# Broadcast of three rstd pairs by DMA through DRAM, the b2 product as one rounded pass, and gate transposes behind the down product

## The reference

```python
xw = x @ Wx + b
h[t+1] = tanh(xw[:, t] + h[t] @ Wh)                  # 32 steps, each on 32 sequences
xf = hs.reshape(-1, 128)                             # 1024 tokens
xn = xf * rsqrt(mean(xf * xf, -1) + 1e-5) * norm_scale
vals, idx = top_k(xn @ wg + bg, 4)                   # 16 experts, 4 chosen
gate_full = sum_k one_hot(idx_k) * softmax(vals)_k
h2 = xn @ w1[e] + b1[e]                              # for every expert e
a, g = min(h2[::2], 7), clip(h2[1::2], -7, 7)
s = a * sigmoid(1.702 * a) * (g + 1)
t = sum_e gate_full[:, e] * (s @ w2[e] + b2[e])
out = x + (hs + t)
```

## Time and profile before

| | |
|---|---|
| timed executions, us | 109.71, 110.6, 113.1 (median 110.6) |
| profiled execution, us | 110.22 |
| its span, first to last instruction, us | 108.4 |
| TensorE busy | 102.9 us, 95% |
| VectorE, ScalarE, GpSimd busy | 64.6, 60.8, 63.8 us |
| DMA | 12.94 MB |

### The profile page before, as it was taken

How to read it: one execution, slowest core, us unless ns; L and a number is a source line. 1 busy time by engine, 2 the same in 40 slices (tenths; PEclk the granted TensorE clock), 3 DMA queues, 4 the chain that set the end, 5 groups by cost and what they waited for, 6 DMA issues and landing times.

```text
span 108.4 us, 1718 instructions
## 1 busy us (share of the span) xinstructions
PE 102.9 (95%) x562; PEld 87.0 (80%) x562; DVE 64.6 (60%) x173; ACT 60.8 (56%) x139; POOL 63.8 (59%) x76
## 2 busy tenths in 40 slices
PE   7899999999999999999999969999999999999980
PEld 2557689988899999999989958886888888888760
DVE  0101367876818976399747996578266656666730
ACT  5144826899646486767716645665364566645400
POOL 3004348987791996449980799896444466545400
PEclk9999999999999999999999999999999999999999
DMA  2997930007930002991058814991000000000012
GB/s 77 235 335 266 398 113 0 0 6 234 390 159 3 0 0 74 296 379 39 12 165 246 308 60 116 336 361 59 6 0 0 0 3 0 0 0 0 0 48 48
DMA packets 4936, 12.94 MB, mean 119 GB/s; under 512 B 752, under 2 KB 1728, under 8 KB 4928
## 3 DMA queue, kind: packets, MB, share of 16 engines
q1 hardware_dynamic: 4704, 12.67, 34.7%
q10 hardware_dynamic: 224, 0.17, 0.6%
HBM read 12.25 MB, written 0.59 MB: 118 GB/s over the span
## 4 chain that ended last, share of the span: by engine, by line
PE 79%; DVE 9%; ACT 5%; DMA 2%; issue 1%; DVEq 0%
PE psA L774 19%; PE psB L774 17%; PE psY L804 10%; PE psR L804 5%; PE psR L722 5%; PE psM L804 5%; PE psY L722 2%; DMA wx_x_sb<-in_wx_x 2%; PE psA L751 2%; PE psM L729 2%; PE psR L714 2%; ACT psA L483 2%; PE psR L816 2%; ACT psA L492 2%; PE psM L816 2%; DVE lin L667 1%
## 5 line engine op out<-in xcount | busy, mean ns | idle before, releaser
L406 POOL TENSOR_TENSOR actg<-act,gate_cols 128x512 f32<-128x512 f32 x31 | 39.4, 1279 | 13.7 <-DVE act L682 12.9
L667 DVE TENSOR_SCALAR lin<-psB,one_b1b 128x256 f32<-128x256 f32 (+1 forms) x48 | 26.0, 569 | 23.3 <-PE psB L774 23.3
L483 ACT ACTIVATE psA<-psA,lim_b1a 128x256 f32<-128x256 f32 (+1 forms) x48 | 23.8, 515 | 26.5 <-PE psA L774 26.5
L682 DVE SCALAR_TENSOR_TENSOR act<-lin,psA 128x512 f32<-128x512 f32 x32 | 21.9, 686 | 1.8 <-ACT psA L492 0.5
L492 ACT ACTIVATE psA<-psA,limit_col 128x512 f32<-128x512 f32 x32 | 21.1, 660 | 0.8
L774 PE MATMUL psA<-xn_hi,w_hi 128*128 128x256 f32 (+1 forms) x48 | 20.5, 428 | 0.0
L804 PE MATMUL psY<-actg,w_sb 128*128 128x256 f32 x64 | 17.1, 389 | 0.0
L774 PE MATMUL psB<-xn_hi,w_hi 128*128 128x256 f32 (+1 forms) x48 | 16.0, 332 | 0.0
L774 PE MATMUL psA<-xn_hi,w_lo 128*128 128x256 f32 (+1 forms) x48 | 15.8, 328 | 0.0
L774 PE MATMUL psB<-xn_lo,w_hi 128*128 128x256 f32 (+1 forms) x48 | 15.6, 325 | 0.0
L774 PE MATMUL psB<-xn_hi,w_lo 128*128 128x256 f32 (+1 forms) x48 | 15.5, 323 | 0.0
(11 more groups left out here) (82 smaller groups left out, 136.0 us busy)
## 6 DMA issues: line engine op xcount, KB each, us to landing
gate_cols<-gate_rows SPq DMA_DIRECT2D x16, 512.0 KB, 6.0
w_sb<-in_w SPq DMA_DIRECT2D x4, 512.0 KB, 8.0
w_sb<-in_w SPq DMA_DIRECT2D x4, 256.0 KB, 9.3
out<-yT SPq DMA_DIRECT2D x3, 128.0 KB, 1.7
wx_x_sb<-in_wx_x SPq DMA_DIRECT2D x1, 320.0 KB, 6.0
wx_x_sb<-in_wx_x SPq DMA_DIRECT2D x2, 128.0 KB, 2.5
small_h<-in_small ACTq DMA_DIRECT2D x1, 105.0 KB, 2.7
gate_rows<-gT SPq DMA_DIRECT2D x4, 16.0 KB, 1.4
```

The costliest lines, as they stand in the source:

```text
L406: nc.gpsimd.tensor_tensor(by_pair(actg[:, u % SUM_DEPTH, w]), by_pair(act[:, u % ACT_DEPTH, w]), gate_block(u, w), ALU.mult).then_inc(actg ...
L483: last = nc.scalar.activation(psA[u % 2][:, o], psA[u % 2][:, o], ACT.Relu, scale=-1.0, bias=lim_b1a[:, e0 + k:e0 + k + 1])
L667: last = nc.vector.tensor_scalar(lin[:, v % 2, o], psB[v % 2][:, o], one_b1b[:, e0 + k:e0 + k + 1], LIMIT + 1.0, ALU.add, ALU.min)
L682: nc.vector.scalar_tensor_tensor(act[:, v % ACT_DEPTH, 0:w], lin[:, v % 2, 0:w], 1.0 - LIMIT, psA[v % 2][:, 0:w], ALU.max, ALU.mult).then_ ...
```

## The change

Pairs 1 to 3 no longer use TensorE for spreading rstd. SP writes the pair's `rstd` (128 partitions by 2) to DRAM and reads it back with one 128 KB broadcast transfer into `rstd_cols`, ahead of the gate transfers of the same pair. VectorE's `normalise` for these pairs waits for this transfer, reads `rstd_cols` instead of psM, and stands one unit later (`NORMAL` = 7, 11, 15), with GpSimd's `xn_low`.

`b2` is loaded five times below itself (80 rows), on ScalarE's queue behind `small`. VectorE makes a rounded copy and, in the last 16 rows, a remainder. The gates are written three times side by side, 80 columns wide with zeros between, so that the transposes give 80 rows; ScalarE makes a second, rounded copy `gS`, VectorE replaces 16 rows of it by the remainder (`gates_low`), and one float32r product with 80 rows of contraction takes the place of the float32 product.

From unit 7 on the gate transposes stand behind the down product of their unit. The filler products between the steps of the head are gone (five of 512 columns at the start stay); the logits of tile 0 move between steps, and the product of x and Wx for tiles 3 and 4 becomes two products, one in front of `lay_rstd(1)`. The last four units' down products are split 384 and 128 columns instead of 256 and 256, with the additions and the stores split alike, and the first half of the last one waits for both gate products.

```diff
@@ -41,7 +41,7 @@
...
     NU = UNIT0[NC]
-    WARM, WARM_START, WARM_GAP = 512, 5, 256
+    WARM, WARM_START = 512, 5
     LAG = 4
...
@@ -62,11 +62,14 @@
...
     RSTD = [None] + [v + 1 for v in STATS[1:]]
+    NORMAL = [None] + [v + 3 for v in STATS[1:]]
     GATES, GATES_T = [[k] + [v + 2 + k for v in STATS[1:]] for k in (0, 1)]
...
     EQ = E // GATE_GROUPS
+    GR = 5 * E
+    LOW_AT = 32
...
@@ -90,7 +93,8 @@
...
         bg_sb = sb("bg_sb", [P, E])
-        b2_sb = sb("b2_sb", [E, H])
+        b2_sb = sb("b2_sb", [GR, H])
+        b2_w = sb("b2_w", [GR, H], F32R)
         w1_sb = sb("w1_sb", [H, E, 2, I])
...
@@ -234,9 +248,10 @@
...
-        def y_end_bank(k):
-            return psM if k else psR
+        def y_end(k):
+            o = [slice(0, 3 * P), slice(3 * P, W)][k]
+            return o, (psM if k else psR)[:, 0:o.stop - o.start]
...
@@ -284,7 +299,7 @@
...
                 g = pair_group(q)
-                later += [(STATS[q], 1, ("stats", g)), (RSTD[q], 2, ("rstd", g))]
+                later += [(STATS[q], 1, ("stats", g))]
             order += [k[2] for k in sorted(later, key=lambda k: k[:2])]
...
@@ -305,7 +320,6 @@
...
                 sp.dma_start(w2_sb[:, ge, :], w2[:, ge, :]).then_inc(w2_loaded[g], 16)
-            sp.dma_start(b2_sb[:, :], b2).then_inc(b2_loaded, 16)
...
@@ -320,13 +334,24 @@
...
+            def spread_rstd(q):
+                sp.wait_ge(rstd_ready, pair_group(q) + 1)
+                sp.dma_start(rstd_rows[q, :, :],
+                             rstd[:, 2 * q:2 * q + 2]).then_inc(rstd_written, 16)
+                sp.wait_ge(rstd_written, 16 * q)
+                sp.dma_start(rstd_cols[:, q, :], rstd_rows[q, :, :].rearrange("p j -> (p j)")
+                             .partition_broadcast(P)).then_inc(rstd_loaded[q], 16)
             for q in range(NQ):
+                if q:
+                    spread_rstd(q)
                 spread_gates(q)
...
             for k in range(2):
-                o = slice((NT - 4 + 2 * k) * P, (NT - 2 + 2 * k) * P)
+                o = slice((NT - 1) * P if k else (NT - 4) * P, NT * P if k else (NT - 1) * P)
                 sp.wait_ge(yT_ready, NC + k)
...
@@ -349,6 +374,7 @@
...
             nc.gpsimd.memset(expo[:, :, 0:1], 1.0)
+            nc.gpsimd.memset(gates_w[:, :, :], 0.0)
             nc.gpsimd.iota(iota_e[:, :], pattern=[[1, E]], base=0, channel_multiplier=0,
...
@@ -417,7 +443,7 @@
...
             for v in range(NU - 1 + POOL_LAG):
-                for q in at(RSTD, v - 1):
+                for q in at(NORMAL, v):
                     xn_low(pair_group(q))
...
@@ -433,6 +459,7 @@
...
             acte.dma_start(small_h[:, 0:SM], small).then_inc(small_loaded, 16)
+            acte.dma_start(b2_sb[:, :], b2).then_inc(b2_loaded, 16)
             acte.wait_ge(ident_ready, 1)
...
@@ -455,7 +482,9 @@
...
                 acte.wait_ge(gates_mm, q + 1)
-                nc.scalar.activation(gT[:, q * PW:(q + 1) * PW], psX[0:E, 0:PW], ACT.Copy).then_inc(gT_ready, 1)
+                qc = slice(q * PW, (q + 1) * PW)
+                nc.scalar.activation(gT[:, qc], psX[0:E, 0:PW], ACT.Copy).then_inc(gT_ready, 1)
+                nc.scalar.activation(gS[:, qc], psX[0:GR, 0:PW], ACT.Copy).then_inc(gS_high, 1)
...
@@ -501,7 +530,7 @@
...
             acte.wait_ge(yT_ready, NC + 1)
-            store(acte, slice((NT - 2) * P, NT * P), slice(P // 2, P))
+            store(acte, slice((NT - 1) * P, NT * P), slice(P // 2, P))
...
@@ -531,18 +560,25 @@
...
+                if g >= CHUNKS[0]:
+                    q = group_tiles(g).start // 2
+                    dve.wait_ge(rstd_loaded[q], 16)
+                    nc.vector.scalar_tensor_tensor(xn[:, group_cols(g)].rearrange("p (j t) -> p j t", j=2),
+                                                   hT[:, group_cols(g, N)].rearrange("p (j t) -> p j t", j=2),
+                                                   b_col[:, 1:2],
+                                                   rstd_cols[:, q, :].rearrange("p (t j) -> p j t", j=2),
+                                                   ALU.mult, ALU.mult).then_inc(xn_full, 1)
+                    dve.wait_ge(xn_full, q)
+                    nc.vector.tensor_copy(xn_hi[:, group_cols(g)], xn[:, group_cols(g)]).then_inc(xn_hi_ready, 1)
+                    return
                 m = psM_turn(("rstd", g))
...
                 h, n = hT[:, group_cols(g, N)], psM[:, 0:len(group_tiles(g)) * P]
-                if g < CHUNKS[0]:
-                    nc.vector.scalar_tensor_tensor(xn_hi[:, group_cols(g)], h, b_col[:, 1:2], n, ALU.mult,
-                                                   ALU.mult).then_inc(xn_hi_ready, 1)
+                nc.vector.scalar_tensor_tensor(xn_hi[:, group_cols(g)], h, b_col[:, 1:2], n, ALU.mult,
+                                               ALU.mult).then_inc(xn_hi_ready, 1)
                 nc.vector.scalar_tensor_tensor(xn[:, group_cols(g)], h, b_col[:, 1:2], n, ALU.mult,
...
                 dve.wait_ge(m_read, m)
-                if g >= CHUNKS[0]:
-                    nc.vector.tensor_copy(xn_hi[:, group_cols(g)], xn[:, group_cols(g)]).then_inc(xn_hi_ready, 1)
-                    return
                 dve.wait_ge(xn_hi_ready, g + 1)
...
@@ -607,14 +643,31 @@
...
                 nc.vector.tensor_tensor(
-                    gates[:, ts, :], gate_sum[:, ts, :],
-                    inv[:, ts].rearrange("p (j o) -> p j o", o=1).to_broadcast([P, 2, E]),
+                    gates_w[:, ts, :].rearrange("p j (a b e) -> p j a b e", a=3, b=2)[:, :, :, 0, :],
+                    gate_sum[:, ts, :].rearrange("p j (a e) -> p j a e", a=1).to_broadcast([P, 2, 3, E]),
+                    inv[:, ts].rearrange("p (j a e) -> p j a e", a=1, e=1).to_broadcast([P, 2, 3, E]),
                     ALU.mult).then_inc(scale_done, 1)
+            def gates_low(q):
+                dve.wait_ge(gS_high, q + 1)
+                low, qc = slice(LOW_AT, LOW_AT + E), slice(q * PW, (q + 1) * PW)
+                nc.vector.tensor_tensor(gS[low, qc], psX[low, 0:PW], gS[low, qc].bitcast(F32),
+                                        ALU.subtract).then_inc(gS_ready, 1)
...
                 gates_scale(q)
+            def b2_parts():
+                dve.wait_ge(b2_loaded, 16)
+                mark(nc.vector.tensor_copy(b2_w[:, :], b2_sb[:, :]))
+                settled()
+                low = slice(GR - E, GR)
+                nc.vector.tensor_tensor(b2_w[low, :], b2_sb[low, :], b2_w[low, :].bitcast(F32),
+                                        ALU.subtract).then_inc(b2_ready, 1)
...
@@ -634,6 +687,7 @@
...
             nc.vector.tensor_scalar(one_b1b[:, :], b1_sb[:, E:2 * E], 1.0, None, ALU.add).then_inc(b1_ready, 1)
+            b2_parts()
             stats(0)
...
@@ -667,6 +721,8 @@
...
                     last.then_inc(lin_done, 1)
+                for q in at(GATES_T, v - 1):
+                    gates_low(q)
                 for q in at(STATS, v):
...
@@ -696,10 +752,10 @@
...
             for k in range(2):
-                dve.wait_ge(y_end, k + 1)
-                o = slice((NT - 4 + 2 * k) * P, (NT - 2 + 2 * k) * P)
-                nc.vector.tensor_tensor(yT[:, o], xT[:, o], y_end_bank(k)[:, 0:PW],
-                                        ALU.add).then_inc(yT_ready, 1)
+                dve.wait_ge(y_done, k + 1)
+                o, y = y_end(k)
+                o = slice((NT - 4) * P + o.start, (NT - 4) * P + o.stop)
+                nc.vector.tensor_tensor(yT[:, o], xT[:, o], y, ALU.add).then_inc(yT_ready, 1)
...
@@ -708,10 +764,10 @@
...
-            def x_wx(j, n):
+            def x_wx(j, n, start=True):
                 pe.wait_ge(x_loaded if j > 2 else x1_loaded if j else wx_x0_loaded, 16)
-                nc.tensor.matmul(xw_cols(j, n), wx_sb, xT[:, j * P:(j + n) * P], start=True, stop=True,
+                nc.tensor.matmul(xw_cols(j, n), wx_sb, xT[:, j * P:(j + n) * P], start=start, stop=True,
                                  skip_group_check=True)
...
@@ -731,7 +787,8 @@
...
-                for k, j in enumerate(ts):
+                for j in ts:
+                    k = j % 2
                     last = nc.tensor.matmul(bank[:, 16 + k * E:16 + (k + 1) * E], hT[:, N + j * P:N + (j + 1) * P],
...
@@ -745,7 +802,7 @@
...
-            def keep_warm(n, w=WARM_GAP):
+            def keep_warm(n, w=WARM):
...
@@ -753,9 +810,9 @@
...
                 if q:
-                    pe.wait_ge(gT_ready, q)
+                    pe.wait_ge(gS_ready, q)
                 for k, j in enumerate(pair_tiles(q)):
-                    last = nc.tensor.transpose(psX[0:E, k * P:(k + 1) * P], gates[:, j, :], ident[:, :])
+                    last = nc.tensor.transpose(psX[0:GR, k * P:(k + 1) * P], gates_w[:, j, 0:GR], ident[:, :])
                 last.then_inc(gates_mm, 1)
...
@@ -779,21 +836,21 @@
...
                     return [(slice(0, CHUNKS[c] * P), psY[:, 0:CHUNKS[c] * P])]
```

(55 more changed lines are left out.)

7 lines of the change are left out of this document (5 added, 2 removed).

## The result

The changed kernel took 117.47 us in the median (116.14 to 120.34, 4 runs), the kernel before beside it 110.17 (109.71 to 113.1, 4 runs). The ratio is 1.060 with a 95% interval of 1.054 to 1.067: slower by 6%, outside the forecast range of 108.2 to 112.6. Executions more than 1.5% above the fastest of their kernel, mostly those with a lower granted clock, are left out of every ratio, which is why this one is under the 1.066 of the two medians. The profiled execution took 116.14 us for a span of 114.4, the same 1.7 us around the span as before. So 6.0 us of span are to be found.

What follows compares the result with a forecast made beforehand. TensorE was taken as the bound, busy 102.9 of 108.4 us. Span 108.4 + 1.6 (wait) - 0.66 (chunk 2) - 0.2 (tail) = 109.15, with 1.8 around it 110.95, given as 110.9; range 108.2 to 112.6 us.

Steps and rivals of the forecast that it cites:

- The head: Head to unit 1: part of x by Wx runs earlier, the gS copy adds 0.27; net +0.1 us, summed as -0.1 gain.
- b2: Chunks 0, 1 and 2: one float32r product replaces the float32 product, gaining 0.3, 0.3 and 0.66 us.
- Transposes behind the down product: The two TensorE stops ending at 50.78 and 63.23: moving the gate transposes gains 0.1 us at both places.
- Sum up to unit 16 without the wait: TensorE up to unit 16: gains of 0.5 + 0.3 + 0.25 = 1.05 us, so a start at 63.4, before 64.48.
- the 0.25 of the last pair: Unit 13: two rstd transposes less on TensorE, 0.25 us at most.
- The tail: Last units: smaller last addition (0.13 us less) and a last store half as large, 0.2 us together.
- The new wait: Before unit 16: pair 3's rstd write lands after pair 2's gate columns drain, rstd_cols at 65.0; 1.6 us lost.
- Pair 2 has the same wait, shorter: Unit 11: rstd_cols at about 51.2, VectorE ready at 50.9 at the earliest; the loss is made up by unit 12.
- A: SP's rstd write overtakes the gate columns: unit 16 waits only 0.25 us for xn_lo; 108.5 us, chance 0.25.
- B: Head without fillers: the clock rises two units later, or idling before unit 16 does the same; 112.6 us, chance 0.15.
- C: Wait longer or repeated: rstd(2) holds the addition before chunk 1's product, 8-byte write adds 0.8; 1.3 more, 112.2 us, chance 0.1.
- D: The 80-row float32r product shows the old one's price: 1.2 us less gain, 111.7 us, chance 0.05.

Runs made afterwards that it cites:

- both edits: Changed kernel with the rstd write as one 1 KB piece and the read from 128 rows of x, other data than asked for: 111.17 us, one run.

## Why the prediction was wrong

*The parts of the gain.* *The head*: +0.1 net. The kernel with the old head equals the one without within the intervals, which neither bears out nor refutes 0.1. *b2*: 0.3, 0.3 and 0.66. Chunk 2 gave 0.82 in its products (0.84 + 0.22 became 0.18 + 0.06), more than 0.66, since the start cost that I kept was mostly not there. The two 0.3 brought unit 16 forward by nothing: it starts at 63.68 without the rounded pass too. *Transposes behind the down product*: 0.1, and nothing measurable came. *Sum up to unit 16 without the wait*: 63.4; with transposes, which keep the 0.25 of the last pair, it was 63.68. That this fits is luck in part, since 0.6 of the 1.05 us in the sum is b2. *The tail*: 0.2. From the tail's first product to the end of the span it was 108.4 - 101.64 = 6.76 us and is 114.4 - 108.02 = 6.38. 0.4, a little under-sized.

*The new wait* was the right mechanism, on the right queue and in the right order, but it was put at the wrong pair. What failed is one sentence: "Pair 2 has the same wait, shorter", `rstd_cols` "at about 51.2", and that what it loses "is made up by unit 12". It is 56.8. Of the 5.6 us between them, 2.4 are the write: I let it land when the gate columns had drained, but they were through soon after 50 and it landed at 52.66; its 128 pieces had a bound of 0.8 in pair 3's working and none here. 1.95 are the read, 4.15 where I took 2.2 from the 2.5 us row of a load with 128 rows of its own. That row was nearest by size, but it reads neither one row 128 times nor behind such a write, and each adds some 1 us. The remaining 1.2 is the drain itself: `gate_rows` of pair 1 landed after 3.4 us instead of 1.4, so the gate columns were issued at 43.23 instead of 41.86.

*What followed from it I had not followed.* VectorE was ready for `xn` of pair 2 at 51.8. With `rstd_cols` at 51.2 it waits for nothing; with 56.8 it waits 5.0, and the first product of chunk 1 came at 59.53 instead of the 54.0 of the text. The clock fell. And everything of pair 3 moved with it, its statistics and its `rstd` (ready at 61.78 where the text has 55.56), its routing and the gate products. So the wait that the forecast was built on, 1.6 us lost at `rstd_cols` of pair 3, hardly occurred: VectorE stood there for 0.15 us. Two paths end almost together before unit 16. The gate product ended at 70.44; `rstd_cols` of pair 3 landed at 66.25 + 3.8 = 70.05, which with `xn` and `xn_hi` makes 71.05. `xn_lo` needs both, so the second one decides, by 0.6 us. The kernel with pair 2 normalised late shows the forecast wait alone: there VectorE stands for 5.8 us at pair 3, whose `rstd_cols` land at 69.83 where the text has 65.0, and unit 16 starts at 70.72.

*Why the write is late* was put down to its place in SP's queue, and with it went the sentence of the Trainium skill, "DMA: Bandwidth & Descriptors", section "Queues, rings and completion order", on ring order. The write on ScalarE's empty queue was held for 6.3 us as well. Ring order may act on SP too, where the write took 7.6, but most of the hold is there without it. The same page's fixed cost and bandwidth ("Anatomy of one DMA", a fit that the page made on DMAs issued by GpSimd, where these are SP's) give 4.3 us for the round trip as an estimate. The emptiest one here, pair 1, took 2.7 + 4.3 = 7.0, and the form with one piece and own rows took 1.1 + 2.0 = 3.1. So the rule fits neither form. With the bytes the same, the pieces alone moved the round trip from 3.9 (1.1 + 2.8) to 7.0.

*The rivals.* A is refuted in two steps: the write is held up, and on an idle queue the round trip would have brought pair 3's `rstd_cols` at 55.7 + 0.7 + 7.0 = 63.4 and not at 60.0. B did not occur as told: the pace of the up products rose at 18.3 us, in the kernel before at 19.9. That the clock can fall over an idle stretch, which B adds for the stop before unit 16, did occur, one stop earlier; in other kernels of this case it occurred there too, and cost 2.9 us. C named what happened ("`rstd(2)` is late enough to hold the addition before chunk 1's product") and had the 0.8 for the pieces, but it was priced at 1.3 us where it cost 5.05 in the first stop and 7.4 by unit 16, and it had a chance of 0.1. D is refuted by the float32 variant (its own terms, 0.3 + 0.66 on top of 110.9, make 111.9 and not the 111.7 of the text). The range went wrong by the same sum: the upper bound came from one late pair, not from the second pair and the queue behind it.

## What to carry to other kernels

A small round trip through DRAM is not priced by its bytes: price it by its pieces, and by whether large transfers are in flight while it runs. Here 1 KB and 128 KB took 7 us on an idle queue and up to 12 beside 2 MB. The clock is a second price: a stop can cost some 3 us more in the products behind it than its own length. Before putting one into a loop, work out for each of its turns when it lands and what stands behind its wait on every engine in order, SP too; the turn that looked harmless here was the one that had less slack than its wait was long. And where a change has several parts, find the part that pays: here one product form gave 1.6% and the large part took 8 back.

## What the runs showed of the hardware

- A 1 KB write to DRAM landed after 1.1 us as one piece and 2.7 to 3.1 as 128 pieces of 8 bytes, and the 128 KB read behind it took 1.0 to 1.5 us longer when the write had been in pieces (4.3, 4.2, 3.8 against 2.8, 3.0, 2.8; 3.1 against 2.0), even where it read other data. Why the read is longer is open.
- A write issued within 2 us of 2 MB of gate columns took 5.8 to 7.9 us, whatever its form, and 6.3 and 5.9 from another engine's empty queue. Issued 3.5 to 5 us behind them it took 4.3 to 4.8.
- `gate_rows` of pair 1, 16 KB, landed after 1.4 us before, with transposes and in their three variants, and after 2.1 to 3.5 in the kernels with the DMA path. It isn't issued behind a large transfer there. Left open; that of pair 0 took about 3 us in three profiles, one of them with transposes, so the DMA path need not be the reason.
- The granted clock reads 1.00 in the head, where six up products take 1.30 us; in the one-piece kernel six take 1.28 in windows that read 0.50. The first up product at the faster pace begins between 17.9 and 20.5 us in the thirteen profiles without fillers in the head (18.6 in the changed kernel), and between 19.5 and 20.4 in the three with them, so the fillers don't bring it forward.
- After a stop of 1.0 us in the one-piece kernel the granted clock fell in one profile, with both edits, after one of 0.9, it did not. Where it fell in the stop before unit 16, the rest of the span took 44.3 to 45.4 us instead of 42.5.
